# Routing first: tokens sorted by their chosen head on the chip, and routed keys and values formed for sorted tiles

## The reference

```python
xn = layernorm(x)
# local attention: 16 query heads, 4 key/value heads of width 32, window of 64 earlier tokens
q, k, v = xn @ Wq.T + bq, xn @ Wk.T + bk, xn @ Wv.T + bv
q, k = rope(rmsnorm(q, qn_w)), rope(rmsnorm(k, kn_w))
local = softmax(masked(q k^T * scale)) v @ Wo.T + bo
# routed attention: 16 query heads, one shared key/value per token, causal over 1024 keys
gating = softmax(xn @ W_gate.T);  idx = argmax(gating)          # one of 16 heads a token
fq, fk, fv = split(xn @ W_qkv.T, 3)                             # each 512 wide = 16 heads x 32
k_shared = fk[head idx];  v_shared = fv[head idx] * max(gating)
routed = softmax(causal(fq k_shared^T / sqrt(32))) v_shared
out = x + local + routed
```

## Time and profile before

| | |
|---|---|
| three runs | 687.32, 684.36, 686.43 us; median 686.43 |
| span of the profiled execution | 684.4 us |
| PE / DVE / ACT / POOL busy | 94% / 73% / 53% / 65% |
| token stage | 0 to about 400 us |
| routed stage | about 400 to 684.4 us |

### The profile page before, as it was taken

One profiled execution on the slowest core, in us unless ns is written; L12 is line 12 of the kernel. 1 busy time (PEld: TensorE's weight loads), 2 busy tenths in 40 slices (PEclk: granted clock), 3 DMA queues, 4 the chain that ended last, 5 costly groups with the idle time before them and its releaser, 6 DMA issues.

```text
span 684.4 us, 19451 instructions
## 1 busy us (share of the span) xinstructions
PE 646.0 (94%) x7432; PEld 510.2 (75%) x7432; DVE 496.3 (73%) x1328; ACT 362.5 (53%) x906; POOL 442.6 (65%) x368
## 2 busy tenths in 40 slices
PE   3788999999999899999899899999999999999997
PEld 3577888887788688888688667777777777777775
DVE  3956966677678866787676368888888787879454
ACT  4436444472527344445335555556566566656674
POOL 3965764938195735684487267685868777778730
PEclk9979999999999999999999999999999999999999
DMA  8522213231232032222214541321314131402011
GB/s 295 206 59 86 82 38 115 86 98 51 66 102 61 30 112 70 64 70 74 77 32 118 158 142 56 96 64 50 111 49 110 51 106 32 110 28 87 4 33 33
DMA packets 64942, 56.61 MB, mean 83 GB/s; under 512 B 6481, under 2 KB 48849, under 8 KB 64849
## 3 DMA queue, kind: packets, MB, share of 16 engines
q1 hardware_dynamic: 62704, 54.45, 27.2%
q10 hardware_dynamic: 2144, 0.93, 0.5%
HBM read 37.20 MB, written 17.89 MB: 80 GB/s over the span
## 4 chain that ended last, share of the span: by engine, by line
PE 78%; DVE 9%; POOL 4%; ACT 3%; issue 2%; DMA 2%; ACTq 1%; DVEq 0%; POOLq 0%
PE gemm L938 17%; PE s_ps L1047 12%; PE od_ps L1096 11%; PE st_ps L1080 10%; PE gemm L1024 6%; PE od_ps L1110 5%; PE win L998 3%; PE gemm L934 3%; PE win L983 2%; PE s_ps L1119 2%; DMA rope_t<-rope 2%; PE av L1010 2%; DVE l_sum L1266 2%; ACT p_loc L1492 2%; DVE l_max L1257 1%
## 5 line engine op out<-in xcount | busy, mean ns | idle before, releaser
L938 PE MATMUL gemm<-w_tok,xt 128*128 128x512 f32 (+1 forms) x768 | 186.1, 384 | 3.3 <-DVE x_res L1283 0.9
L938 PEld LDWEIGHTS gemm<-w_tok,xt 128*128 128x128 f32 x768 | 131.7, 193 | 28.2 <-issue 1.4
L1318 DVE CUSTOM_DVE_ANT_0 s_ps<-s_ps,x_ln 128x512 f32<-128x512 f32 (+3 forms) x224 | 127.6, 620 | 24.4 <-PE s_ps L1047 24.0
L1047 PE MATMUL s_ps<-k_stack,w_tok 96*128 96x512 f32 (+2 forms) x336 | 101.5, 385 | 0.3 <-DVE x_res L1283 0.3
L1080 PE MATMUL st_ps<-w_tok,k_stack 98*128 98x512 f32 x288 | 99.0, 413 | 0.2 <-ACT p_loc L1540 0.2
L1540 ACT ACTIVATE p_loc<-st_ps 128x512 f32<-128x512 f32 x144 | 77.7, 599 | 36.0 <-PE st_ps L1080 34.8
L1634 POOL TENSOR_TENSOR rope_b<-qkv,sin_t 128x128 f32<-128x128 f32 (+1 forms) x32 | 27.5, 880 | 79.5 <-DVE qkv L1232 79.3
L1047 PEld LDWEIGHTS s_ps<-k_stack,w_tok 96*128 96x128 f32 x336 | 55.0, 188 | 28.3 <-DVE picked_fk L1318 12.4
L1492 ACT ACTIVATE p_loc<-win,l_max 128x96 f32<-128x96 f32 x256 | 60.9, 391 | 19.1 <-DVE l_max L1257 19.0
L934 PE MATMUL gemm<-xt,w_qt 128*128 128x256 f32 x384 | 57.1, 293 | 6.3 <-DVE picked_fv L1211 3.5
L1540 ACT ACTIVATE p_loc_t<-st_ps 128x512 f32<-128x512 f32 x96 | 52.4, 599 | 19.8 <-PE st_ps L1080 19.3
(11 more groups left out here) (172 smaller groups left out, 1298.7 us busy)
## 6 DMA issues: line engine op xcount, KB each, us to landing
w_tok<-q_parts SPq DMA_DIRECT2D x72, 128.0 KB, 2.6
q_parts<-qt SPq DMA_DIRECT2D x120, 64.0 KB
x_ln<-x SPq DMA_DIRECT2D x8, 512.0 KB, 4.7
x_res<-x SPq DMA_DIRECT2D x16, 256.0 KB, 2.9
partial<-x_res SPq DMA_DIRECT2D x16, 256.0 KB, 2.6
w_tok<-partial SPq DMA_DIRECT2D x8, 512.0 KB, 5.2
raw<-w_tok SPq DMA_DIRECT2D x3, 1024.0 KB, 12.9
v_win<-v_rows SPq DMA_DIRECT2D x64, 48.0 KB, 2.2
```

The costliest lines, as they stand in the source:

```text
L938: i = e.matmul(g[:, 0:cols], xs[l][:, k, a * P:(a + 1) * P], w_tok_p[r][:, k, c0:c0 + cols], start=first, stop=last)
L1047: e.matmul(s_ps[bank][:, 0:cols], q_op[b][0:HALVES, i, h, :], k_stack[0:HALVES, b * S + c0:b * S + c0 + cols], start=True, stop=True).then ...
L1318: e.tensor_tensor_reduce(out=s[:, 0:cols], in0=s[:, 0:cols], in1=causal[:, S - width + c0:S - width + c0 + cols], scale=1.0, scalar=dst if ...
```

## The change

All 16 tiles are normalised, turned and gated first. x gets four buffers, with loads ahead. The normalised x and its turned halves go to DRAM (`normed`, `turned`); q and qt read the turned halves back (`xtb`), and are held until the sixteenth kvg product has been issued (`AHEAD`). Keys and values go to DRAM together (`kv_rows`), and the keys of a tile come back before its rope.

The heads' weights for fk and fv, 64 columns by 512 rows for each of 16 heads, are loaded, split into two halves and stored (`experts`). When all tiles are gated, two fp32 matmuls with a triangle and with ones count, for each token, the earlier tokens of its head (`rank`); DVE turns that into a row number (`place`), where every head begins at a multiple of 64 rows: at most 47 half tiles, 24 tiles. POOL scatters the rows of xn by 16 indirect DMAs into `x_sorted`, which was filled with zeros. For each of the 24 sorted tiles SP reads the heads of its two halves from `eid` into a register and loads the rows and the two heads' weights; PE turns the tile and multiplies it with both heads' columns (8 matmuls of 256 columns); DVE adds the high and low part for the right half of the rows (`kv_sorted`, stored). 16 indirect DMAs on POOL pick each token's key and value back in token order, and the old split and turn follow. The first maxima come after that.

Beside this, rmsnorm's power on POOL becomes a logarithm and an exponential on ACT with one Newton step on DVE (three small instructions). `choose` lets the planner take the first of 8 queued products that is ready. Six weight pieces become four, each with its own buffer.

```diff
-PIECES = ("kvg", "q", "fk", "fv", "qt", "wo")
-UNITS = [("kvg", 0), ("q", 0), ("fk", 0), ("kvg", 1), ("fv", 0), ("qt", 0), ("qt", 1), ("q", 1), ("fk", 1),
-         ("fv", 1), ("qt", 2), ("qt", 3)]
+PIECES = ("kvg", "q", "qt", "wo")
+UNITS = [("q", 0), ("qt", 0), ("qt", 1), ("q", 1), ("qt", 2), ("qt", 3)]
...
+HT = P // 2
+HALF_TILES = TOK // HT + H - 1
+SORTED = -(-HALF_TILES // 2)
+FILLS = 4
+E_PIECE = 2
+PICKS = 8
+LOOK = 8
+AT_ONCE = 4
+LOADS = 4
+AHEAD = (16,) * ROUNDS
+X_BUFS = 4
...
+    def reload():
+        for n in range(ROUNDS):
+            while n not in stored or stored[n] > p.now or n > 1 and n - 2 not in rounds_done or len(valued) < AHEAD[n]:
+                yield None
+            do("xt_load", n)
+            held[n] = p.now + X_LANDS
+            yield 0, []
...
+    def dispatch():
+        for group in range(2):
+            do("xg_load", group)
+        while not bank_ready():
+            yield None
+        freed = take_bank(("rank",), ("gemm_read", "rank"))
+        do("rank")
+        yield 1.0, []
+        do("place")
+        yield 0, [("V", 6.0)], freed
+        for group in range(TILES // AT_ONCE):
+            for t in range(AT_ONCE):
+                do("scatter", group * AT_ONCE + t)
+            if group >= 2:
+                yield 0, [("", 1.0)]
+            yield 0, [("G", 1.4 * AT_ONCE)]
+            if group + 2 < TILES // AT_ONCE:
+                do("xg_load", group + 2)
+        yield 0, [("", 2.5)]
+        for s in range(LOADS):
+            do("sorted_load", s)
+            sorted_in[s] = p.now + 6.0 + 2.0 * s
+        p.add(sort_turned())
...
+    def picks():
+        do("routed_rooms")
+        p.rooms = True
+        for group in range(0, TILES, PICKS):
+            for t in range(group, group + PICKS):
+                do("pick", t)
+            yield 0, [("G", 1.4 * PICKS), ("", 1.0)]
+            for t in range(group, group + PICKS):
+                yield from take_pick(t)
...
+            elif step == "expert":
+                s, = key
...
+                lane.wait_ge(*M["st_lo"].of(s))
+                for kc in range(KC):
+                    for l in range(2):
+                        i = e.matmul(g, xst[s % 2][l][:, kc, :], w_ex[s % LOADS][:, :, kc, :], start=kc + l == 0,
+                                     stop=kc + l == KC)
...
                 lane.wait_ge(*M["gemm_mm"].of((n, "kvg", a)))
                 if n:
-                    lane.wait_ge(*M[f"v_out{a}"].of(n - 1))
-                    lane.wait_ge(*M["k_t_mm"].of((n - 1, a)))
-                e.tensor_tensor(qkv[a][:, HD:N_QKV], g[:, 0:KV], bias[:, HD:N_QKV], ALU.add).then_inc(
+                    lane.wait_ge(*M[f"kv_out{a}"].of(n - 1))
+                e.tensor_tensor(kv_a[a][:, :], g[:, 0:KV], bias[:, HD:N_QKV], ALU.add).then_inc(
...
+            elif step == "place":
...
+                lane.wait_ge(*M["rank_mm"].of("all"))
+                lane.wait_ge(*M["table_in"].of("all"))
+                lane.wait_ge(*M[f"xt_out{(ROUNDS - 1) % 2}"].of(ROUNDS - 1))
...
+            elif step == "e_split":
+                n, = key
+                lane.wait_ge(*M[f"e_in{n % 2}"].of(n))
+                if n:
+                    lane.wait_ge(*M["e_out"].of(n - 1))
+                e.activation(e_halves[:, :, :, 0:E_COLS].bitcast(F32R), e_raw[n % 2][:, :, :, :], ACT.Copy).then_inc(
+                    *M["e_hi"].did(n))
...
                 if n >= 2:
-                    lane.wait_ge(*M["gemm_mm"].of((n - 2, *LAST_UNIT)))
+                    lane.wait_ge(*M["gemm_mm"].of((n - 2, "kvg", 1)))
+                    lane.wait_ge(*M[f"xt_out{n % 2}"].of(n - 2))
...
+                e.activation(rms_e[:, :], rms_v[:, :], ACT.Ln).then_inc(*M["rms_e"].did(("log", n, a)))
+                lane.wait_ge(*M["rms_e"].of(("log", n, a)))
+                e.activation(rms_e[:, :], rms_e[:, :], ACT.Exp, scale=-0.5).then_inc(*M["rms_e"].did((n, a)))
...
+            elif step == "scatter":
...
+                e.indirect_dma_start(out=x_sorted[:, :], out_offset=bass.IndirectOffsetOnAxis(
+                    ap=slot[:, t:t + 1], axis=0), in_=xg[group % 2][:, at, :], in_offset=None).then_inc(
+                        *M[f"scat{group % 2}"].did(group, inc=16))
...
+            elif step == "sorted_load":
...
+                if s >= LOADS:
+                    lane.wait_ge(*M["gemm_mm"].of(("expert", s - LOADS)))
+                e.dma_start(xs[s % LOADS][:, :], x_sorted[s * P:(s + 1) * P, :]).then_inc(
+                    *M[f"sort_in{s % LOADS}"].did(s, inc=16))
+                for h in range(2):
+                    who = e.value_load(eid[0:1, 2 * s + h:2 * s + h + 1], min_val=0, max_val=H - 1)
+                    e.dma_start(w_ex[s % LOADS][:, h, :, :].rearrange("p k c -> p (k c)").bitcast(F32),
+                                experts[bass.ds(who, 1), :, :].rearrange("o p c -> (o p) c")).then_inc(
+                                    *M[f"sort_in{s % LOADS}"].did(s, inc=16))
```

More of the change, by code:

```diff
@@ L1 @@
+import itertools
 import concourse.bass as bass
@@ L144, in busy, with choose @@
         return start
+    def choose(self, ready):
+        best = None
+        for n, product in enumerate(itertools.islice(self.products, LOOK)):
+            at = ready(product)
+            if at is not None and (best is None or max(at, self.now) < best[0]):
+                best = max(at, self.now), n
+        if best is None:
+            return None
+        product = self.products[best[1]]
+        del self.products[best[1]]
+        self.products.appendleft(product)
+        return best[0]
     def run(self, ready):
@@ L192, in win_ready, with bank_ready @@
         return all(win_free[g] is not None and win_free[g] <= p.now for g in banks)
+    def bank_ready():
+        free = bank_free[banks[0]]
+        return free is not None and free <= p.now
     def take_bank(step, release):
@@ new lines, in sort_turned, with turned, expert, ready @@
+    def sort_turned():
+        for s in range(SORTED):
+            while s not in sorted_in or sorted_in[s] > p.now or s > 1 and s - 2 not in placed:
+                yield None
+            p.take("tp1", ("sorted_t", s), ("st_lo", s))
+            do("sorted_t", s)
+            def turned(end, s=s):
+                split[s] = end + HOP
+                ahead(expert(s))
+            yield 0.45, [("A", 0.6), ("V", 0.7)], turned
+    def expert(s):
+        def ready():
+            return None if bank_free[banks[0]] is None else max(bank_free[banks[0]], split[s])
+        def multiply():
+            freed = take_bank(("expert", s), ("gemm_read", ("expert", s)))
+            do("expert", s)
+            placed.add(s)
+            if s + LOADS < SORTED:
+                do("sorted_load", s + LOADS)
+                sorted_in[s + LOADS] = p.now + 7.0
+            p.add(take_expert(s, freed), 0.95 + HOP)
+        return ready, [(0.95, multiply)], "expert"
@@ L347, in attend @@
             yield 0, [("A", 1.2)]
-        while not win_ready(*range(HKV)) or m and (m - 1, a) not in p.transposed or pieces_made[0] < len(PIECES):
+        while not win_ready(*range(HKV)) or m and (m - 1, a) not in p.transposed:
             yield None
@@ L450, in make_plan @@
     do("x_load", 0)
-    for n in range(RAWS):
-        do("w_load", n)
-    do("late_constants")
-    p.add(normalise(0), X_LANDS)
+    do("w_load", 0)
+    for n in range(1, X_BUFS):
+        do("x_load", n)
+    do("w_load", 1)
+    do("w_load", 2)
+    do("late_constants")
+    do("w_load", 3)
+    for n in range(2):
+        do("e_load", n)
+    p.add(statistics(), X_LANDS)
+    p.add(turn())
+    p.add(pieces())
+    p.add(reload())
+    for a in range(2):
+        p.add(keys(a))
     p.add(first_maxima())
@@ L774, in mixed_attention_kernel @@
+    causal = sb(one, "causal", [P, S])[:, :]
+    r_max_s = sb(one, "r_max_s", [P, 2, P], F32R)
+    big = sb(one, "big", [P, 2 * SORTED * H])
     over = ExitStack()
[L775 removed]
+    raw = [sb(over, f"raw{n}", [P, KC, COLS[kind][1]]) for n, kind in enumerate(PIECES)]
     rope_t = sb(over, "rope_t", [P, S // P, 2, DK])
@@ L909, in tensor_program @@
                 n, kind, a, kc = key
-                g, xs = gemm[plan.turn["bank", ("gemm", n, kind, a)]], xt[n % 2]
+                g, x2 = bank_of("gemm", n, kind, a), xta[n % 2] if kind == "kvg" else xtb[(n + 1) % 2]
                 if kc == 0:
```

795 lines of the change are left out of this document (516 added, 279 removed).

## The result

The changed kernel takes 829.9 us (median of three, 827.8 to 830.5) against 686.4. The ratio is 1.209, with a 95% interval from 1.205 to 1.213. The profiled execution spans 829.2 us.

The account below looks back on a forecast made before the run. PE was taken to bound the token stage: T 100 us, 287.5 us of PE work at 0.96 and a 4 us tail end it at 391.5 against 400, so 686.4 less 8.5 gives 678 us, range 658 to 706.

Parts of the forecast that it names:

- T: End of the gating pass over all 16 tiles, before the held-back q products; taken as 100 us, between 85 and 112.
- PE's work: Token stage: 367 us less 89 plus 39 gives 317 us, of which 276 us at full clock come after T.
- The last stage: Routed attention from 400 us on, untouched by the change: 284 us carried over.
- the queue doesn't run dry: Gating pass: reason to assume 370 GB/s for the remaining 28.5 MB of DMA traffic, 77 us more.
- The rival with a throttled pass: Gating pass: engines wait for its own stores to land, T 115 to 121 us, total 695 up to 701 us; chance 0.24.
- The fast rival: Gating pass: DVE, not DMA, is the limit, T is 86 us, total 665 us; chance 0.18.
- The density of 0.96 after T: Token stage after T: PE busy 0.96 of the time, so 276 us of work take 287.5 us.
- No engine is over 0.75: Token stage after T: attention's win banks 208 and DVE 214 of 290 us, offered in support of PE's density of 0.96.
- the tail: End of the token stage, 380 to 400 us, last tile's attention alone: 4 us of idle PE, kept.
- The rival that named the mechanism: Token stage: the routed chain sets the end, sum 321 to 370 us against 385; if it decides, 701 us; chance 0.16.
- hidden under PE's products as long as two tiles are under way: Each tile's attention chain, where the 58.6 us power on POOL gives way to two small ACT and three small DVE instructions.
- The indirect DMAs: 16 scatters and 16 picks on POOL, charged 1.4 us each, 45 us; far more would make the number wrong.

Follow-up runs that it names:

- half of the stores: Changed kernel without SP's stores of the routed queries' low halves, the high half being read twice: 808.9 us.
- first loads from POOL: Changed kernel with the loads of the first four sorted tiles issued by POOL behind the last scatter instead of by SP: 825.0 us.
- zeros late: Changed kernel with the four stores of zeros into the sorted rows moved behind the sixteenth kvg product: 843.0 us.
- power on POOL: Changed kernel with rmsnorm's power back on POOL, and the plan charging it as before: 849.3 us.
- one pair's q products early: Changed kernel with the first pair of tiles' q and qt products let into the first pass once five tiles have their keys: 837.9 us.
- replanned: Changed kernel, same work, with an order planned for the later landings of tokens, scatters, sorted tiles and query stores that the trace shows: 845.8 us.
- 16 tiles: Changed kernel with the last eight of its 24 sorted tiles neither loaded, transposed nor multiplied: 811.4 us.
- free maxima: Changed kernel with the chain kept, but the 48 first maxima multiply early available output weights instead of waiting for keys and queries: 804.5 us.

## Why the prediction was wrong

It gave 678 us and a range of 658 to 706. The result is 124 us above the range and 152 above the number. The stage ends at 543.6 and not at 391.5 us: 16 of these 152 us lie before T, 136 behind it.

- **PE's work** was right. The 39 us added and 89 us removed gave 276 us after T; the trace has 272 by the estimate at full clock. The last stage was carried over at 284 and is 284.
- **T** was taken as 100 and is 115.6 us. The rate of full DMA engines was right, 375 GB/s against the 370 assumed, but they are full only from 60 us on; in the 60 us before they moved 290 GB/s. The premise that "the queue doesn't run dry" failed there. The last kvg product comes at 106.6 us, within the bounds of the DMA estimate, and 9 us more go by until the first q product. The rival with a throttled pass had T at 115 to 121, and that came true, with both of the signs that it named, ACT before `e_halves` and DVE before `kv_a` on a DMA:

```profile
ACT e_halves L1687 <- DMA experts<-e_halves: 19.3, 5, 7.1
DVE kv_a L1394 <- DMA kv_rows<-kv_a: 11.5, 6, 4.4
```

How much of T these waits make was not measured; taking 16.8 us of transfers out moved T by 8.5. The fast rival, T at 86 us by DVE's work, did not show in any run.
- **The density of 0.96 after T is the step that failed.** "No engine is over 0.75" was true and said nothing. The density was asked from each engine's sum of work, and the new stage is not bound by a sum. It came out as 0.63 at full clock: from T to the stage's end there are 156 us over the work, where 11.5 were allowed for and 4 more for the tail. About 49 of them are work stretched by a lower granted clock (321 us of busy time for 272 of work), and some 107 are idle PE.
- **The rival that named the mechanism was mis-sized in every term.** It said that the routed chain sets the end, and gave it 321 to 370 us against 385, so it cost nothing unless 20 us late. Its terms and what they measured: place 6 (9, counted from T to the first scatter), scatters 30 (53), from there to the first expert nothing (45), experts 70 (112), and from the last expert to the last maximum 55 + 60 (188: 37 and 150). From T to the last maximum that is 406 us and not 221 (270 at its upper end), and 22 more go by until the stage ends. Of the missing 45 us, 32 lie ahead of the first load in SP's order, behind stores of q; with that load issued by POOL, where it stands 19 us behind the last scatter, 7.5 came back. Each expert was costed by what its four buffers allow, 2.5 to 3 us, and takes 4.7. In these tiles ACT waits 38.7 us for their transposes on PE, which stand there between q products and attention, and PE waits 17.6 us for the heads' weights to land; which of the two sets the 4.7 was not tested.
- **Bringing the power from POOL to ACT and DVE was costed at nothing**, as "hidden under PE's products as long as two tiles are under way". That failed too: alone it costs the kernel before about 40 us. In the changed kernel it is worth keeping (19 us); without the chain it costs 14, so it is the chain on POOL that makes it pay.
- **The indirect DMAs** were said to break the number if far over 1.4 us. They take 0.96 and 0.94 us on POOL.

By experiment the 143 us divide so, from the bottom up, as far as one order of steps shows it: 7 us stay with neither chain nor split root (the rest of the change, less the work that went), 14 us come with the split root, 123 with the chain. Added in the other order the parts are different: the split root alone is 40, and with the chain there it gives 19. Inside the 123: 25 for the maxima at its end, 18 for a third of the experts; and half of the stores that SP and ACT must get past are worth 21. These overlap and weren't tried together. How far the first expert product's start carries to the end, in us:

| kernel | first expert | stage end | between |
|---|---|---|---|
| changed | 222.5 | 543.6 | 321 |
| half of the stores | 202.1 | 521.4 | 319 |
| first loads from POOL | 215.0 | 538.9 | 324 |
| zeros late | 227.8 | 556.7 | 329 |
| power on POOL | 229.9 | 561.7 | 332 |
| one pair's q products early | 233.5 | 551.4 | 318 |
| replanned | 250.4 | 558.5 | 308 |
| 16 tiles | 218.3 | 521.4 | 303 |
| free maxima | 221.3 | 517.9 | 297 |

With the same work behind it (the first seven rows) the end moves the same way as the start in all six variants, by 0.5 to 2.5 times as much. An experiment that shortens a link gives back less than the link's length: 22 of 31 us, 25 of 150. So it is not a single chain of latencies. The chain's steps and the remaining q and attention steps sit in the same engines' fixed orders, and the waits above show either kind standing behind the other. How the rest of the 123 us is shared between the chain's own latency and the fill that it holds up stays open, as does what a full clock throughout would have given; no run held the clock up without changing the order. No variant beats the kernel before.

## What to carry to other kernels

A change that puts a data-dependent barrier into a stage where everything ran side by side (all tokens gated, then sorted, then multiplied, then picked) has to be costed as a chain of latencies, each link with the queue in which its instructions and DMA issues stand; an engine's sum of work is only a floor. Look at in-order queues that are nobody's bottleneck: SP issued the chain's first load 32 us after the last scatter, behind stores at 0.74 us each, and POOL, given the same load, issued it after 19. And moving work off a busy engine is only a gain if that engine releases someone; here 58.6 us left POOL, and the time rose by 40 us in the kernel before.

## What the runs showed of the chip

- A row scatter of 128 rows of 2 KB by indirect DMA holds POOL for 0.96 us and lands 4.7 us after its issue; a gather of 128 rows of 256 B holds it for 0.94 us and lands after 3.9 us:

```profile
x_sorted<-xg,slot POOLq DMA_INDIRECT x16, 4.7
chosen<-kv_sorted,slot POOLq DMA_INDIRECT x16, 3.9
```

- Full DMA engines moved 375 GB/s over 55 us. The Trainium skill, "DMA: Bandwidth & Descriptors", section Specifications, gives about 358 GB/s for what HBM feeds one core; the trace doesn't agree with that as a ceiling over a long stretch either.
- Where PE had gaps, the mean granted clock was below full. In the windows above it is 0.75 to 0.77 in the pass, where PE works 51.5 of 115 us, 0.72 from 115 to 200 us (54.7 of 85), 0.81 from 340 to 545 us (154.5 of 205), and 0.96 from 200 to 340 us (112.2 of 140). These are means between its two levels, 1.2 and 2.4 GHz. From 545 us on, with PE busy 277.7 of 284 us, it is 1.00. So idle time was paid twice here: 272 us of work took 321 us of busy time behind T.
